# Two experts ahead instead of one: splitting weights in the last stage of a two-layer transformer kernel

## The reference

```
x2   = layernorm(src)                          # 2 x 1024 rows of 128
sel  = sigmoid(x2 @ sel_w)                     # 32 experts
gate = the four largest of sel, 0 elsewhere
h    = relu(einsum('bsd,edh->bseh', x2, keys)) # keys:   32 x 128 x 128
moe  = einsum('bseh,ehd,bse->bsd', h, values, gate)   # values: 32 x 128 x 128
out  = src + moe
```

## Time and profile before

| what | value |
|---|---|
| median of three runs | 2306.72 us |
| the profiled execution | 2307.15 us |
| its span, first to last instruction | 2305.4 us |
| PE busy over the span | 2110.5 us (92%) |
| DVE, ACT, POOL busy over the span | 1574.1, 1256.5, 585.5 us |
| first key product of expert 2 starts | 2114.83 us from the span's start |
| first key product of expert 31 starts | 2288.41 us |

### The profile page before, as it was taken

How to read it: one execution, slowest core, us unless ns; L and a number is a source line. 1 busy time by engine, 2 the same in 40 slices (tenths; PEclk the granted TensorE clock), 3 DMA queues, 4 the chain that set the end, 5 groups by cost and what they waited for, 6 DMA issues and landing times.

```text
span 2305.4 us, 44523 instructions
## 1 busy us (share of the span) xinstructions
PE 2110.5 (92%) x14656; PEld 1308.9 (57%) x14656; DVE 1574.1 (68%) x2113; ACT 1256.5 (55%) x2193; POOL 585.5 (25%) x561
## 2 busy tenths in 40 slices
PE   4799999689984999999499999999999999976998
PEld 2344444367762344443267777777777777754776
DVE  4799998456655999995656666566666666655666
ACT  1588888256641788887244444444444444433443
POOL 1000000268861000000132222222222222213554
PEclk8799999599996899999799999999999999987999
DMA  7344443221105444442510000011000000013554
GB/s 235 111 124 106 121 112 81 64 100 64 46 1 166 102 106 122 110 116 70 156 31 24 24 24 24 24 31 29 24 24 24 24 24 24 25 50 126 200 190 159
DMA packets 87433, 185.35 MB, mean 80 GB/s; under 512 B 17808, under 2 KB 50576, under 8 KB 81936
## 3 DMA queue, kind: packets, MB, share of 16 engines
q1 hardware_dynamic: 87376, 184.64, 27.8%
HBM read 149.84 MB, written 36.57 MB: 81 GB/s over the span
## 4 chain that ended last, share of the span: by engine, by line
PE 40%; issue 5%; POOL 3%; DVE 2%; DMA 1%; SPq 1%; ACT 0%; POOLq 0%; DVEq 0%; ACTq 0%
PE PS L713 18%; PE PS L547 10%; PE PS L742 5%; PE PS L708 4%; PE PS L698 2%; POOL BIG_r L1643 2%; POOL PR_r L1637 1%; PE PS L768 1%; DMA rope<-r_dram 0%; PE PS L568 0%; DVE st L909 0%; DVE xn L921 0%; DMA Qs<-g_dram 0%; DMA Ws_r<-w_stack 0%; DMA q_stack<-hl 0%
## 5 line engine op out<-in xcount | busy, mean ns | idle before, releaser
L1101 DVE TENSOR_REDUCE M<-PS 128x1 f32<-128x1024 f32 x512 | 605.8, 1220 | 71.8 <-PE PS L612 67.6
L1363 ACT ACTIVATE PR<-PS 128x512 f32<-128x512 f32 x1024 | 535.9, 589 | 125.1 <-PE PS L632 124.3
L1120 DVE TENSOR_REDUCE M<-PS 128x1 f32<-128x1024 f32 x256 | 313.5, 1225 | 236.1 <-PE PS L713 236.1
L632 PE MATMUL PS<-Qs_r,Ks_r 32*128 32x512 f32 x1024 | 370.8, 505 | 1.7 <-ACT PR L1363 1.2
L1391 ACT ACTIVATE BIG<-PS 128x512 f32<-128x512 f32 x256 | 153.0, 598 | 334.6 <-PE PS L547 334.6
L642 PE MATMUL PS<-PR,Va 128*32 128x256 f32 x4096 | 322.0, 399 | 0.0
L612 PE MATMUL PS<-Ks_r,Qs_r 32*128 32x512 f32 x1024 | 266.6, 517 | 44.1 <-DVE hl L1023 17.3
L632 PEld LDWEIGHTS PS<-Qs_r,Ks_r 32*128 32x128 f32 x1024 | 152.1, 185 | 250.8 <-ACT PR L1363 178.0
L1380 ACT ACTIVATE PR<-PS,M 128x1024 f32<-128x1024 f32 x256 | 284.9, 1113 | 12.3 <-DVE M L1120 12.3
L547 PE MATMUL PS<-ident,PR 128*128 128x128 f32 x2080 | 273.1, 275 | 3.7 <-DVE PR L1232 1.9
L547 PEld LDWEIGHTS PS<-ident,PR 128*128 128x128 f32 x2080 | 240.2, 141 | 51.0 <-issue 21.3
(11 more groups left out here) (161 smaller groups left out, 2822.1 us busy)
## 6 DMA issues: line engine op xcount, KB each, us to landing
Qs_r<-q_stack SPq DMA_DIRECT2D x320, 128.0 KB, 2.6
Ks_r<-k_stack SPq DMA_DIRECT2D x320, 128.0 KB, 3.0
Qs<-g_dram SPq DMA_DIRECT2D x30, 1024.0 KB, 4.7
o_dram<-Ob SPq DMA_DIRECT2D x96, 128.0 KB, 2.3
Ks<-g_dram SPq DMA_DIRECT2D x10, 1024.0 KB, 4.7
q_stack<-hl SPq DMA_DIRECT2D x36, 256.0 KB, 3.0
k_stack<-hl SPq DMA_DIRECT2D x36, 256.0 KB, 3.9
Ks<-in_kv SPq DMA_DIRECT2D x32, 128.0 KB, 2.1
```

Source lines behind the costliest of these rows:

```text
L632: e.matmul(bank(RING[(x if x < 4 else x + 1) % 3]), Ks_r[rows_, s, kt * P:(kt + 1) * P], Qs_r[rows_, s, qh * GW:(qh + 1) * GW], start=True ...
L1101: e.tensor_reduce(M[:, s, qt:qt + 1], PS[:, 2 + 2 * (qt % 2):4 + 2 * (qt % 2), :] .rearrange("p a b -> p (a b)"), AX.X, ALU.max, negate=Tr ...
L1120: e.tensor_reduce(M[:, s, qt:qt + 1], PS[:, 2 * (qt % 2):2 * (qt % 2) + 2, :] .rearrange("p a b -> p (a b)"), AX.X, ALU.max, negate=True). ...
L1363: e.activation(PR[:, kt % 4, qh * GW:(qh + 1) * GW], bank(RING[(x if x < 4 else x + 1) % 3]), ACT.Exp, scale=SCALE).then_inc(exp_done, 1)
```

## The change

ACT and POOL split the weights of two experts ahead of the first one (`weights(0)`, `weights(1)`), and then, while expert `x` runs, those of expert x + 2 instead of x + 1. POOL still does this behind its two low parts of expert `x`. ACT does it behind the high part of group 1 instead of behind that of group 0. The slots of `wsp` are taken as before, and the last two experts split nothing. The code of PE, DVE and SP is the same.

```
@@ ScalarE, experts1
                 def unit(i, s, tg, last=False):
                     v = NG * (SLOTS * i + s) + tg
                     high(v, tg)
-                    if tg == 0 and not (last and s == SLOTS - 1):
-                        weights(SLOTS * i + s + 1, (s + 1) % SLOTS, 2 * i + (s + 1) // 2)
+                    if tg == 1 and not (last and s >= SLOTS - 2):
+                        weights(SLOTS * i + s + 2, (s + 2) % SLOTS, 2 * i + (s + 2) // 2)
 
                 weights(0, 0, 0)
+                weights(1, 1, 0)
@@ GpSimd, experts1
                     if not last:
-                        weights(x + 1, (s + 1) % SLOTS)
+                        weights(x + 2, (s + 2) % SLOTS)
 
                 weights(0, 0)
+                weights(1, 1)
@@
                 for s in range(SLOTS):
-                    expert(NE1 - SLOTS + s, s, s == SLOTS - 1)
+                    expert(NE1 - SLOTS + s, s, s >= SLOTS - 2)
```

## The result

| | us |
|---|---|
| kernel before, median of 15 launches (range) | 2309.96 (2304.53 to 2315.57) |
| changed kernel, median of 15 launches (range) | 2294.42 (2289.69 to 2305.2) |
| ratio, 95% interval | 0.9942 (0.9931 to 0.9954) |
| profiled execution of the changed kernel | 2300.92, its span 2299.1 |

The change makes the kernel faster, by 13.4 us by the ratio (0.0058 x 2309.96; interval 10.6 to 15.9) and by 15.5 between the medians. The forecast was 2290.8. The median is 3.6 above it, inside the range. But the median of the 15 launches of before in the same comparison lies 3.2 above that of the three that the forecast was anchored on (2306.72; the three are among the 15), and the ratio times their median, 0.9942 x 2309.96 = 2296.6, is above the range's upper end of 2295.5.

What follows compares the result with a forecast made beforehand. A loop through POOL's weight split, queued behind the low parts, was taken to set 6.00 us per expert. At 5.44, 15.8 + 0.0 + 0.1 = 15.9 us gained gave 2290.8; range 2288.8 to 2295.5.

Steps and rivals of the forecast that it cites:

- The level: Whole kernel: gain of 15.9 us taken from the profiled execution's 2307.15, then 0.4 lower for the median shown: 2290.8.
- The loop: Stage of 32 experts: period per expert falls from 6.00 to 5.44 us, 29 periods taking 157.8 instead of 173.58.
- A rest at each border: Rival: unit 0 of each expert on PE keeps 1.49 us, period 5.57, 3.8 us lost, 2294.6; chance 0.13.
- the loop's branch: PE's loop branch, seven times, uncovered could cost 0 to 3.0 us; taken as 0.
- ACT's move to group 1: ACT's split behind group 1's high part ends at 4.1, next high part not before 4.30: cover 0.2 us.
- SP's queue and the DMA engines: Weight loads issued earlier against their use, lead 8.8 us, cost nothing; DMA engines at 219 GB/s have room.
- The start: Stage's start: ACT held by expert 2's weights eats the earlier split's gain, 0.0; rival, ACT not held, 1.6 better, chance 0.05.
- The weights of expert 3 behind those of expert 2: Stage's start: expert 3's weights issued right behind, 0.3 us later if their 128 KB shared the way.
- The end: Behind the start of expert 31 only unit 0's refill changes: -0.1 us.
- Faster matmuls: Rival: PE matmuls take 0.216 us each instead of 0.227, time 2283.3; chance 0.02.
- Slower, ACT held in every expert: Rival: ACT waits for weight loads throughout the loop; at 12 us landing 6.6 per expert, +18, 2325; chance 0.03.

Runs made afterwards that it cites:

- The doubled split: POOL's weight split done twice, first result unused: in the kernel before 2331.17 us, ratio 1.0102; in the changed kernel 2289.35 us, ratio 0.9903.
- the second execution: Profiled execution of the changed kernel run again with no edit; median 2294.83 us over 8 launches, ratio 0.9945 to the kernel before.
- the changed kernel's third execution: Profiled execution of the changed kernel run a third time with no edit; median 2289.02 us over 6 launches, ratio 0.9912 to the kernel before.
- the kernel that loads first: Changed kernel with SP loading expert 2's weights ahead of the wait for gate writes and the gate rows; median 2294.34 us, ratio 0.9939.
- that with one expert ahead: Kernel before, split still one expert ahead but before group 0's high part on ACT and both low parts on POOL; 2293.93 us, ratio 0.9943.
- that with group 0: Changed kernel with ACT's split put back behind the high part of group 0; median 2294.16 us, ratio 0.9936.
- the quarter rows: Changed kernel with expert 2's weights loaded first and expert 0's gate row in four quarter loads; 2289.59 us, ratio 0.9912; again 2291.06, 0.9927.
- before's second profiled execution: Profiled execution of the kernel before run once more with no edit; median 2310.42 us over 12 launches, ratio 0.9999 to its other launches.

## Why the prediction was right, and where it was wrong

**The level: wrong, and the step that failed.** "The median shown is 0.4 lower: 2290.8" took the median of three launches within 1.1 us as the kernel's time. Before scatters from 2301.5 to 2317.5 over 68 launches, with a median of 2309.6; the three, which are among the 68, lay 2.9 below that by chance. The sum had no term for it, and the range was built from the change's own bounds only. From 2309.6 the same sum gives 2293.7, and the mean measured is 2294.0. The profile of before warned of it in one place. The page's row of the granted clock, in tenths, cuts the span into 40 slices (9 stands for 90% or more). It falls to 8 and below in several stretches ahead of the stage, which takes some three and a half slices at the end; nothing in three launches of nearly one time says that it always falls there alike.

```profile
PEclk8799999599996899999799999999999999987999
```

**The loop: right.** The period is 5.44, expert 2 to expert 31 took 157.76 (157.8 in the sum), unit 0 takes 1.36. The steps laid out from the first key product came at 0.88, 1.68, 2.39 and 5.00; the prediction had 0.88, 1.68, 2.39 and 5.05. The doubled split shows the cause on both sides: 0.68 per expert before, 0 after. One word of the prediction needs setting right: the loop goes round four engines, PE, DVE, ACT and POOL, not "all five"; SP isn't in it.

**A rest at each border: not so.** All 29 intervals are 5.44, to 0.01, in every kernel that has the split off the path. No fourth expert is longer, so the loop's branch costs nothing, as taken.

**ACT's move to group 1: priced rightly in the loop, too low at the start.** The prediction saw a cover of 0.2 us in the loop and priced the place at nothing. In the loop it is nothing (period 5.44 at either place), and at the start the place behind group 0 costs some 3 us in the one execution that shows it, since a held ACT then keeps the high part of group 1 too.

**SP's queue and the DMA engines: right.** 217 GB/s at a share of 0.61 in the loop (219 forecast), and no engine waits for a load there.

**The start: 0.0 was near in sum, its steps held only in part.** ACT was held 3.45 us (3.4 forecast) and expert 2 started 18.25 after g (17.9 forecast). But the gap of 1.5 us on PE near 2110 shows in the second execution only, with 0.89. In the first, PE had already stood 3.11 us for the first value product, and then its clock fell, a term that the sum didn't have. That the sum came out all the same is partly luck. Over all executions the start took 18.25 to 19.20 in the changed kernel (mean 18.6) and 17.93 and 19.92 in before (mean 18.9), so the term can't be told from 0 within 1 us.

**The weights of expert 3 behind those of expert 2: no delay seen.** The load of expert 2 took 8.2 to 8.6 us where the weights of expert 3 are issued later and 8.2 to 8.8 where they are right behind; at that scatter the bound of 0.3 is neither excluded nor needed. The Trainium skill's page "DMA: Bandwidth & Descriptors", section "Queues, rings and completion order", says that each DMA engine takes descriptors in ring order; the landings don't contradict it, but their scatter is larger than the 0.3 that it bears on.

**The end: about right.** 16.77 to 16.87 in the changed kernel against 16.93 and 16.99; 0.1 to 0.2 where -0.1 was taken.

**Faster matmuls: not so.** 1.36 for six in every unit, 0.227 each.

**Slower, ACT held in every expert: not so.** In the loop ACT's split waits for nothing.

## What to carry to other kernels

When an engine with much idle time stands in the chain, add up the round trip from the first instruction that it releases back to itself: the period here was a path through four engines, closed by the order of one queue. Such a loop is opened by moving the preparation of the next round in that queue, ahead of this round's work or a round earlier, and either gives the same; doubling the suspected instruction on both kernels tells in two runs whether it is on the loop.

A gain of under one per cent is better read as a distance between two marks in the trace than as a difference of whole times, and the level of a forecast needs the scatter of the kernel's launches, which three of them can hide.

## What the runs showed of the hardware that I had not expected

The whole time goes with the granted clock of the launch. From 0.935 to 0.944 before falls by 13.4 us and the changed kernel by 16.8 (few launches at either end), about as much as the change is worth. Where it comes from lies ahead of the stage: g lay between 2092.15 and 2106.32 in the twelve profiled executions, though all execute the same instructions up to there. Over the first 500 us the granted clock was 0.87 to 0.91, but the delay doesn't arise there alone: the changed kernel's first execution is 22 matmuls behind its second at 500 us, 45 at 1000 and 101 at 1500. Why the clock falls in one launch and not in another at the same instructions was not settled.

At the start of the stage PE's clock fell in some executions and not in others. Windows of the changed kernel's first profiled execution, of 2 us each (columns as in the earlier trace rows):

```profile
2114.00:2116.00 2.00, 0.00 (x0) 0.00 (x0) 2.00 (x4) 1.23 (x2) 0.62 (x1) 1.00 1.05 442
2116.00:2118.00 2.00, 1.29 (x3) 1.10 (x4) 0.45 (x1) 0.00 (x0) 1.88 (x2) 0.64 0.97 406
2118.00:2120.00 2.00, 2.00 (x6) 1.52 (x6) 0.00 (x0) 0.65 (x2) 0.15 (x1) 0.50 0.41 139
2120.00:2122.00 2.00, 2.00 (x10) 1.51 (x9) 1.71 (x3) 1.13 (x3) 0.59 (x1) 1.00 0.14 47
```

PE had stood still for 3.11 us; then it was granted 0.50, which is 1.2 GHz, and went back to 1.00 by 2120. In between a window of 2 us holds 6 matmuls instead of 10. The same came behind 2.85 to 2.91 us of standing still in the changed kernel's third execution, in the kernel that loads first, in that with one expert ahead and in that with group 0. It didn't come where PE had stood 0.73 to 1.38 at the same place: in the profiled executions of before, of the changed kernel's second, of its doubled split, and of the quarter rows. In all of these PE had been at half clock as the stage began (the eight matmuls ahead of the key products took 5.3 to 6.7 us, against 3.67 in the execution above) and began its key products late, 5.5 to 7.0 us after g against 3.94, and so had less to wait for. One execution fits neither group: with the split doubled in the kernel before, PE began late too, stood 0.74 us there, and its clock fell behind a later rest of 1.63 us. Which rest brings the fall was not settled.

What the quarter rows give at the start can be read apart from the clock, by comparing only executions of the changed order in which it didn't fall: expert 2 began 18.47 and 18.02 us after g (the second execution, the doubled split) against 15.98 and 16.69 with the load first and the quarter rows, so 1.3 to 2.5 us are theirs without the clock. Whether they also keep the clock from falling can't be said, as PE began late in both of their executions. That the fall is nothing of the change shows in before's second profiled execution, where PE had stood 3.32 us:

```profile
2112.00:2116.00 4.00, 3.03 (x9) 2.11 (x8) 1.01 (x3) 0.13 (x1) 1.40 (x2) 0.68 0.42 156
```
